# One call moved down in TensorE's program: side work goes ahead of the transposes of a flipped scan step

## The reference

```python
def _selective_scan(x, dt, Bm, Cm, A, D):          # x, dt: L x 512; Bm, Cm: L x 16
    dA = jnp.exp(dt[..., None] * A)
    dBx = (dt * x)[..., None] * Bm[:, :, None, :]
    def step(h, inputs):
        dA_t, dBx_t, C_t = inputs
        h = dA_t * h + dBx_t
        y = jnp.einsum('bdn,bn->bd', h, C_t)
        return (h, y)
    ...
    return jnp.swapaxes(ys, 0, 1) + x * D[None, None, :]
x = x + attn(cond(x, cond_8))       # attn: convolution, this scan forward and reversed, gate, projection
x = x + ffn(cond2(x, cond_8))       # ffn: eight experts, the best two for each token
```

## Time and profile before

| | |
|---|---|
| median of 3 runs | 1389.91 us (1387.33 to 1390.06) |
| the profiled execution's time | 1389.91 us |
| its span, first to last instruction | 1388.1 us |
| TensorE / VectorE / ScalarE / GpSimd busy | 88% / 65% / 56% / 66% |
| first stage, the scan steps | from about 40 to 912 us |
| second stage, the experts | from about 950 us to the end |

### The profile page before, as it was taken

The page is one execution under the profiler, slowest core; times in us unless marked ns, Lnnn a source line. Parts: engine busy times, 40 slices in busy tenths (PEclk is TensorE's granted clock), DMA queues, the critical chain, the costliest instruction groups (busy, mean ns, idle before and its releaser), DMA issues. The chain is left out here.

```text
span 1388.1 us, 20902 instructions
## 1 busy us (share of the span) xinstructions
PE 1228.0 (88%) x7120; PEld 933.0 (67%) x7120; DVE 899.6 (65%) x1065; ACT 777.4 (56%) x1477; POOL 918.5 (66%) x511
## 2 busy tenths in 40 slices
PE   8978878989788879797787879898999999999997
PEld 3445555656556556566556644467999999999996
DVE  3998999899899899899998889963111111111110
ACT  4787887788887697788886675613111111111111
POOL 1998999999999989999998879822222222222211
PEclk9999999999999899899998799999999999999999
DMA  5665556465556455556555554608988898888982
GB/s 196 216 182 183 168 184 176 156 202 192 176 171 198 152 184 165 183 171 192 186 184 182 178 155 152 194 4 301 369 309 322 318 322 313 310 320 317 323 306 46
DMA packets 109979, 296.95 MB, mean 214 GB/s; under 512 B 10017, under 2 KB 21922, under 8 KB 94386
## 3 DMA queue, kind: packets, MB, share of 16 engines
q1 hardware_dynamic: 100226, 277.53, 57.9%
q0 software_dynamic: 9648, 18.09, 6.5%
HBM read 277.76 MB, written 9.96 MB: 207 GB/s over the span
## 5 line engine op out<-in xcount | busy, mean ns | idle before, releaser
L1376 POOL TENSOR_TENSOR arena<-arena 128x1024 f32<-128x1024 f32 x192 | 456.7, 2395 | 53.8 <-DVE arena L1096 38.2
L472 PE MATMUL ps_y<-ident,arena 128*128 128x128 f32 x1840 | 258.5, 289 | 54.0 <-POOL arena L1376 53.3
L472 PEld LDWEIGHTS ps_y<-ident,arena 128*128 128x128 f32 x1840 | 222.2, 148 | 121.8 <-POOL arena L1376 74.3
L1428 POOL DMA_INDIRECT out_x<-arena x39 | 61.8, 1585 | 304.9 <-ACT arena L1024 279.8
L871 ACT ACTIVATE arena<-arena,An 128x512 f32<-128x512 f32 x316 | 218.6, 710 | 0.1
L871 ACT ACTIVATE ps_de<-arena,An 128x512 f32<-128x512 f32 x196 | 134.9, 688 | 146.4 <-DVE arena L1083 140.4
L1310 DVE TENSOR_TENSOR arena<-ps_du,arena 128x512 f32<-128x512 f32 x39 | 27.0, 692 | 227.8 <-PE ps_du L720 227.8
L1360 POOL TENSOR_TENSOR arena<-arena 128x1024 f32<-128x1024 f32 x67 | 160.2, 2391 | 6.7 <-DMA arena<-bc_scratch 6.7
L720 PE MATMUL ps_y<-arena 128*128 128x128 f32 x1248 | 153.4, 276 | 0.8 <-ACT arena L1012 0.5
L720 PEld LDWEIGHTS ps_y<-arena 128*128 128x128 f32 x1248 | 149.6, 193 | 3.2 <-ACT arena L1012 0.8
L1068 DVE TENSOR_TENSOR ps_u<-ps_du,arena 128x512 f32<-128x512 f32 x196 | 136.8, 698 | 22.2 <-DVE arena L1108 10.1
(11 more groups left out here) (238 smaller groups left out, 2009.2 us busy)
## 6 DMA issues: line engine op xcount, KB each, us to landing
arena<-bc_scratch SPq DMA_DIRECT2D x256, 512.0 KB, 4.7
arena<-in_W SPq DMA_DIRECT2D x117, 1024.0 KB
arena<-arena POOLq DMA_DIRECT2D x15, 512.0 KB, 6.0
arena<-in_cd SPq DMA_DIRECT2D x16, 256.0 KB, 5.4
out_x<-arena SPq DMA_DIRECT2D x17, 128.0 KB, 5.0
arena<-in_xT SPq DMA_DIRECT2D x2, 1024.0 KB, 6.3
arena<-in_w2c SPq DMA_DIRECT2D x1, 2048.0 KB, 9.2
diag<-in_dd SPq DMA_DIRECT2D x16, 128.0 KB, 5.1
```

Of the source, the lines that this page charges most:

```text
L472: t = e.matmul(Y[j][:, part], src[:, part], ident[:, :], start=False, stop=stop, is_transpose=True, skip_group_check=True)
L1376: e.tensor_tensor(hc[:, i % NP, :, :], hh[:, i % NH, :, :], c, ALU.mult).then_inc(gp_hc, 1)
L1428: e.indirect_dma_start(out, bass.IndirectOffsetOnAxis(dest[:, i:i + 1], 0), yo[:, i % 3, :], None, compute_op=ALU.add).then_inc(l_add, 16)
```

## The change

In TensorE's loop over the steps the call of `first_u(i)` moves down past `side_work(i)` and `second_u(i + 1)`. Everything else stays, the waits inside the three functions too.

```diff
                 if i + 1 in ROWS_AT:
                     turn_rows(i + 1)
-                if i < NU and flipped(i):
-                    first_u(i)
                 if i < NU:
                     side_work(i)
                 if i + 1 < NU and flipped(i + 1):
                     second_u(i + 1)
+                if i < NU and flipped(i):
+                    first_u(i)
                 if i == NU:
                     out_block(1, 0, 1, both_side, (0, 1))
                 if i >= LAG:
```

## The result

The changed kernel takes 1414.62 us in the median of four runs (1413.41 to 1415.38), the kernel before on the same chip 1389.09 us (four runs). The ratio is 1.0184, with an interval of 1.0167 to 1.0202: slower by 1.8%, 25.5 us. The forecast was 1411 us, in a range of 1396 to 1423. The profiled execution took 1411.67 us, with a span of 1409.9 us; it is 1.7 us shorter than the shortest of the four, so what its trace shows is 21.8 us of difference and not the whole 25.5.

A forecast was written before the change was run, and what follows sets the result against it. VectorE and GpSimd, both nearly full in the first stage's scan steps, were taken as the bound. Passing delays of 22.5 us less a 1.5 us gain made +21 us on 1389.9, so 1411 us, range 1396 to 1423.

The forecast's parts named there:

- The order at step 70: Sign: TensorE shows side work, then the transposes, then VectorE's first scan 0.11 us after them.
- VectorE's wait: Sign: ahead of line 1096, released by TensorE's transposes, it grows from 6 to some 25 us, 6 to some 18 times.
- GpSimd's: Sign: GpSimd's wait for VectorE grows by some 15 to 20 us.
- the end of the first stage: Sign: the scan steps end 20 us later, and the second stage keeps its length.
- The sum: Delays of VectorE's first scans that pass to the end, added over the priced steps: 22.5 us.
- the prices: Per step: side work's length less TensorE's idle time and the first scan's slack; 31 us over 40 steps.
- the steps taken at nothing: Steps 31, 76, 95, 108, 188 and 223: GpSimd's lag covers their delays; otherwise they would add up to 7 us.
- step 207: Price 2.2 us: 3.2 less 0.98 us that VectorE waits for the same side work a little later.
- step 137: Price 1.4 us, at a flipped step whose stretch runs at the lower clock.
- The gain of 1.5 us: Filled TensorE idle time brings its additions earlier and shortens VectorE's waits; taken at 1.5 us, bounds 0 and 14.5.
- TensorE's wait at line 625 shrinks from 24 to about 10: Sign: TensorE's wait to be allowed to start the moved transposes falls from 24 to about 10 us.
- The clock rival: Fewer TensorE waits mean fewer parts at the low clock, so faster: 1383 us at best; chance 0.02.

The follow-up runs named there:

- e9_whole_again: The whole change once more, nothing else, for a second profile, against the kernel before: 1415.83 us, ratio 1.0198.
- e12_not_188: The whole change except that step 188 keeps the old order, against the kernel before: 1414.52 us, ratio 1.0206.
- e1_only_busy: Against the kernel before, the call moves only in the 19 flipped steps without TensorE idle time ahead of the transposes: 1411.58 us, ratio 1.017.
- e2_only_idle: Against the kernel before, the call moves only in the 21 side-work steps with TensorE idle time ahead of the transposes: 1396.07 us, ratio 1.005.
- e5_turns_6_9: Against the kernel before, the call moves only in flipped steps with i % 16 of 6 or 9: 1406.42 us, ratio 1.0152.
- e6_turns_12_15: Against the kernel before, the call moves only in flipped steps with i % 16 of 12 or 15: 1402.62 us, ratio 1.0122.
- e11_turns_15: Against the kernel before, the call moves only in eight flipped steps, each the last of its group of sixteen: 1392.68 us, ratio 1.0041.
- e10_ample: Against the kernel before, the call moves only in 12 steps where TensorE's idle time should hold the side work: 1391.2 us, ratio 1.003.
- e7: Against the kernel before, the transposes go one place up, ahead of an addition, in six steps where VectorE waited for them: 1386.63 us, ratio 1.001.
- e4: Against the kernel before, the transposes go one place up, ahead of an addition, in fifteen steps: 1388.41 us, ratio 1.0011.
- e3: Against the kernel before, the transposes run between the side work's two products, or after all of it where it has one: 1406.69 us, ratio 1.0138.

## Why the prediction came out right, and where it was off

**The mechanism holds.** Side work ahead of the transposes delays VectorE's first scan; GpSimd waits for it; the first stage gets longer and the second doesn't. The order at step 70, VectorE's wait (forecast some 25 us and 18 times, measured 32.7 and 23), GpSimd's (forecast +15 to +20, measured +25.4) and the end of the first stage (forecast +20, measured +22.5) answer to the signs that the prediction named.

**The sum holds at the end of the steps, but not on the way there.** 22.5 us were to pass; the steps end 22.5 and 26.2 us later in two profiles, and the five subsets 19.0, 3.1, 12.2, 7.0 and 3.4 us later against forecasts of 18.7, 3.8, 14.1, 8.4 and 3.0. The first scan of step 127, half way, tells another story. Here it is in the kernel before and in the changed one:

```profile
468.14 1.26 DVE L1096 TENSOR_TENSOR_SCAN ps_u<-arena,hlast,ps_u 128x512 f32<-128x512 f32 x1
```

```profile
484.44 1.26 DVE L1096 TENSOR_TENSOR_SCAN ps_u<-arena,hlast,ps_u 128x512 f32<-128x512 f32 x1
```

| kernel | up to step 127: forecast, measured | from there to the end of the steps: forecast, measured |
|---|---|---|
| the change, first profile | +10.2, +16.3 | +12.3, +6.2 |
| e9_whole_again | +10.2, +16.9 | +12.3, +9.3 |
| e12_not_188 | +10.2, +18.2 | +12.3, +6.2 |
| e1_only_busy | +9.4, +13.1 | +9.2, +5.9 |
| e2_only_idle | +0.8, +7.6 | +3.1, -4.5 |
| e5_turns_6_9 | +8.5, +13.3 | +5.5, -1.1 |
| e6_turns_12_15 | +1.7, +7.2 | +6.7, -0.2 |
| e11_turns_15 | 0, +4.8 | +3.0, -1.4 |
| e10_ample | 0, +4.5 | 0, -6.5 |

In every one the first half costs more than the prices and the second less, by 3 to 8 us each, and the two errors nearly cancel. That the ends agree to a microsecond is in part luck. Some of it may belong to the one profile of the kernel before and not to the prices: e10, e7 and e4, of which no loss was forecast, are 4.5, 4.1 and 3.1 us behind it at step 127 as well, and in five kernels that leave step 31 as it was (e2, e4, e5, e7, e10) VectorE waits 1.05 to 1.24 us there, where that profile has no wait. With one profile of the kernel before this can't be separated.

**Single terms were off, and cancelled.** Of the steps taken at nothing, 188 is late by 3.5 us in both profiles of the change: its step width takes 2.0 us at the lower clock, and TensorE comes late to it after a wait. Steps 31 and 95, also at nothing, wait 1.36 and 2.69 us in the first profile (95 waited 1.09 before), and 31 waits 3.05 in the second. In e1, where step 185 keeps its old order and 188 moves too, there is no wait at 188 (its first scan starts 3.5 us behind that of 187, as in the kernel before), so it needs more than its own move; the prediction weighed each step by the rows of before, where neither was made. On the other side, in the first profile step 207 was priced at 2.2 and VectorE's wait there fell (1.31 to 0.79 us), and step 137, priced at 1.4, cost nothing. Step 207 is the largest single uncertainty: VectorE waits there 0.79 and 4.59 us in the two profiles of the change, 6.02 in e12, 6.15 in e1, 6.01 in e3, 4.24 in e11 and 0.77 in e6. The long waits are where its tile falls into the lower clock: the granted clock of the 4 us ahead of these transposes was 1.00 with 0.79 and 0.77, 0.68 and 0.73 with 4.59 and 4.24, and 0.50 with 6.02 and 6.15.

**The gain of 1.5 us isn't seen.** The step that failed is "TensorE's wait at line 625 shrinks from 24 to about 10": it fell to 17.2. In the steps with side work it did fall, from 14.6 us (the rows add up to this, not to the 13.6 of the prediction) to 3.1; in the flipped steps without side work it rose from 9.6 to 14.4. The waits for GpSimd grew too (45.6 to 52.7 us), and TensorE's idle time over all the scan steps went from 141.1 to 149.8 us (the stretch less its busy time, in the rows above). So filling idle time in one place didn't shorten TensorE's waits as a whole. Nor did VectorE's wait for line 617 shrink (8.2 to 9.6).

**The clock rival** fell, and the sign was the opposite: the mean over the execution went from 0.948 to 0.937. The rule that the prediction cited, from the Trainium skill, "TensorE: Matmul & The Clock Gate", section "HAM oscillation — how this bites in real kernels", asks whether TensorE's waits became fewer. They didn't: its idle time in the scan steps grew by 8.7 us, so these runs don't speak against the rule. Nor do they bear it out: in e10 the clock of the scan steps is 0.94 against 0.93 with 144.8 us of idle time against 141.1. Nor does the clock alone set the loss, though single long waits go with it: in e5 the scan steps have the same 0.93 as before and end 12.2 us later, in e11 they have 0.91, as in the whole change, and end only 3.4 us later.

**What stays open.** Whether the 3 to 4 us at the passage in six of the partial variants (e1, e2, e5, e6, e10, e11) follow from the moved calls, or fall to one execution or another: each kernel has one profile (the whole change two), and other executions have only a time and a mean clock. So the medians of e2, e10 and e11 (+9.6, +5.0, +6.5 us) hold a part whose cause wasn't separated. For the whole change the passage is as before in both profiles (-0.7, -0.8), so its loss doesn't rest on this. A second profile of the kernel before is also missing; it would tell how much of the error at step 127 is its own.

## What to carry to other kernels

In an engine's in-order queue, work put ahead of a short job that another engine waits for costs its full length wherever the queue has no idle time there; price it step by step from the trace, and don't expect the idle time elsewhere to pay it back. A price read at the full clock is a lower bound: a step width took 1.06 or 2.0 us here. When a sum of many prices comes out right, compare it half way too, before trusting the single prices. When small variants disagree with their own step prices, split the execution by stages before explaining the difference, since it may lie where nothing was changed.

## What the runs showed of the hardware

The lower clock can last through 10 us and more in which TensorE has no gap (10.00 of 10.00 us busy at 0.50 in e10; in e4 the 50 us of the passage have a mean of 0.67, for +9.6 us). Whether the passage gets it differs between kernels whose code for it is the same, and what decides it is not known from these runs. The times of one kernel scatter too: 1381 to 1397 us for the kernel before on one chip, and in the twelve executions of e2 1385.64 us, the shortest, came at a mean clock of 0.945 and 1402.78, the longest, at 0.929.
